# Keys and values of the context attentions: two groups at once, each in seven block products

## The reference

```
q = rope(x @ Wq)        # 512 -> 32 heads x 128
k = rope(ctx @ Wk)      # 512 ->  8 groups x 128
v = ctx @ Wv            # 512 ->  8 groups x 128
p = softmax(q @ k.T / sqrt(128) + mask)   # per batch and head, 128 x 128
x = layernorm(x + (p @ v) @ Wo)
```

## Time and profile before

| | us |
|---|---|
| median of 3 runs | 2557.67 |
| lowest and highest | 2549.81, 2559.54 |
| profiled execution, its own time | 2556.09 |
| span of its instructions | 2554.8 |
| PE busy | 2436.9 (95%) |
| DVE busy | 1671.0 (65%) |
| ACT busy | 989.5 (39%) |
| POOL busy | 733.7 (29%) |

### The profile page before, as it was taken

The page is one execution under the profiler, slowest core; times in us unless marked ns, Lnnn a source line. Parts: engine busy times, 40 slices in busy tenths (PEclk is TensorE's granted clock), DMA queues, the critical chain, the costliest instruction groups (busy, mean ns, idle before and its releaser), DMA issues.

```text
span 2554.8 us, 37687 instructions
## 1 busy us (share of the span) xinstructions
PE 2436.9 (95%) x13016; PEld 1542.3 (60%) x13016; DVE 1671.0 (65%) x3133; ACT 989.5 (39%) x3580; POOL 733.7 (29%) x755
## 2 busy tenths in 40 slices
PE   8999999999999798999999999999998999999998
PEld 7865666666655565456666666556664554555554
DVE  3487777777755777677777777565665644445565
ACT  0013444444444366344444434433555412323330
POOL 1037344443322111364344443222221221000002
PEclk9999999999999999999999999999999999999999
DMA  8452233322322266121333222222661020214430
GB/s 177 101 139 73 76 96 99 87 79 79 93 77 83 91 199 200 62 94 60 95 99 98 89 75 79 87 95 86 191 189 61 22 75 30 95 66 153 132 100 33
DMA packets 220382, 249.97 MB, mean 98 GB/s; under 512 B 49792, under 2 KB 165952, under 8 KB 218144
## 3 DMA queue, kind: packets, MB, share of 16 engines
q1 hardware_dynamic: 212128, 218.20, 28.9%
q10 hardware_dynamic: 8064, 29.36, 3.0%
HBM read 161.49 MB, written 85.98 MB: 97 GB/s over the span
## 4 chain that ended last, share of the span: by engine, by line
PE 80%; DVE 11%; ACT 2%; issue 2%; POOL 2%; DMA 2%; SPq 0%; DVEq 0%; ACTq 0%; POOLq 0%
PE banks L752 12%; PE banks L840 12%; PE banks L824 4%; PE banks L902 4%; PE banks L868 3%; PE banks L303 3%; PE banks L720 3%; PE banks L2091 3%; PE banks L733 3%; PE banks L1521 3%; PE banks L2142 3%; PE banks L2431 2%; PE banks L2468 2%; PE banks L2119 2%; PE banks L2161 2%
## 5 line engine op out<-in xcount | busy, mean ns | idle before, releaser
L947 ACT ACTIVATE E_x<-S_x,sm_x 128x128 f32<-128x128 f32 x512 | 199.2, 390 | 304.3 <-DVE sm_x L1121 304.3
L1183 POOL TENSOR_TENSOR QT<-QT,const 128x512 f32<-128x512 f32 x128 | 171.7, 1342 | 427.7 <-DVE turned L1001 427.7
L161 POOL TENSOR_TENSOR norm_spread<-norm_mv,const 128x1 f32<-128x1 f32 x96 | 20.7, 216 | 909.3 <-DVE norm_mv L157 909.3
L752 PE MATMUL banks<-xT,weights 128*128 128x512 f32 x512 | 237.1, 597 | 7.6 <-POOL weights L1178 5.8
L2589 ACT ACTIVATE E_s<-banks,top_s 128x128 f32<-128x128 f32 x512 | 180.0, 379 | 95.8 <-DVE top_s L2696 95.8
L1079 DVE TENSOR_TENSOR x<-banks,x 128x256 f32<-128x256 f32 (+1 forms) x288 | 147.2, 511 | 84.6 <-PE banks L840 78.6
L840 PE MATMUL banks<-weights,OT 128*128 128x256 f32 x768 | 195.1, 384 | 6.3 <-DVE weights L1062 6.3
L840 PEld LDWEIGHTS banks<-weights,OT 128*128 128x128 f32 x768 | 142.8, 191 | 67.9 <-issue 27.9
L954 ACT ACTIVATE OT<-banks 128x512 f32<-128x512 f32 x128 | 76.1, 595 | 258.2 <-PE banks L902 258.2
L1185 POOL TENSOR_TENSOR QT<-QT,turned 128x512 f32<-128x512 f32 x128 | 169.0, 1320 | 10.0
L752 PEld LDWEIGHTS banks<-xT,weights 128*128 128x128 f32 x512 | 95.0, 191 | 116.5 <-issue 105.6
(11 more groups left out here) (320 smaller groups left out, 4908.1 us busy)
## 6 DMA issues: line engine op xcount, KB each, us to landing
scratch_pt<-blocks_x SPq DMA_DIRECT2D x124, 256.0 KB, 2.0
PT<-scratch_pt SPq DMA_DIRECT2D x496, 64.0 KB, 2.0
scratch_latent_pt<-blocks_s ACTq DMA_DIRECT2D x56, 512.0 KB, 3.6
PT_s<-scratch_latent_pt SPq DMA_DIRECT2D x224, 128.0 KB, 3.0
weights<-in_L_xwq SPq DMA_DIRECT2D x64, 256.0 KB, 3.9
weights<-in_L_xwo SPq DMA_DIRECT2D x64, 256.0 KB, 4.3
scratch_latent_pt<-blocks SPq DMA_DIRECT2D x30, 512.0 KB, 2.6
PT<-scratch_latent_pt SPq DMA_DIRECT2D x120, 128.0 KB, 3.0
```

What stands on the lines that cost most here:

```text
L752: mm = PE.matmul(to, left[:, k, head], moving, start=name in ("P1", "P2", "P4", "P5") and k == 0, stop=k == 1, skip_group_check=name in (" ...
L947: ins = AC.activation(head_of(e, j, u), scores_of(s, j, u), ACT.Exp, bias=sm[:, 0, j:j + 1], scale=1.0, accum_out=sm[:, 1, j:j + 1])
L1183: PO.tensor_tensor(four(to), four(to), spread(cos128, 4), ALU.mult).then_inc(*pool_step.one())
```

## The change

Keys and values are made for two groups at once, as a *pair* job: pair n with even n makes the keys of groups n and n+1, with odd n the values of groups n-1 and n. A pair is cut into the same seven products of blocks as the queries, in three jobs p0 (P2, P1), p1 (P5, P6, P3) and p2 (P4, P7). `Wk` and `Wv` come as 4 matrices of 256 columns. POOL makes three sums of the pair's weights (`pair_sums`, four instructions of 256 elements a partition) for every pair, and once in a stage three sums of ctxT (`sums_of_ctx`, four instructions of 1024 elements a partition); the latter changes ctxT in place, which is why ctxT is loaded again ahead of stage 4 and of the feature attention. ACT copies four blocks of a pair (`pair_copy`: one in p0, two in p1, one in p2), DVE adds four. A product of a pair is two matmuls of 512 positions for keys, and four times two of 128 for values. In the diff, `x_exp(u)` and the like count the units done, and the wait on `x_exp` stands ahead of the mask of unit u. Keys are then rotated from SBUF as queries are. The opening makes pairs 0 and 1; group g makes the queries of g+1 and pair g+2. `S` and `blocks` have one buffer in place of two. The diff, cut to its core (moved waits, views and buffer lists are left out):

```
-            if stage == 1:
-                SP.dma_start(ctxT[:, :, :], dram["ctxT"]).then_inc(*ctx_in.one())
+            SP.dma_start(ctxT[:, :, :], dram["ctxT"]).then_inc(*ctx_in.one())
...
-                S = [sbuf(f"S{n}_x{stage}", [P, 4, P], scope) for n in range(2)]
+                S = sbuf(f"S_x{stage}", [P, 4, P], scope)
-                blocks = [sbuf(f"blocks{n}_x{stage}", [P, 4, P], scope) for n in range(2)]
+                blocks = sbuf(f"blocks_x{stage}", [P, 4, P], scope)
...
-                opening = (("k", 0), ("k", 1)) + QUERIES[0]
-                plans = [(1, 1, 2, 2, 1, 0, 1, 0)] + [(2, 2, 1, 2, 1, 1, 1, 0)] * (G8 - 2)
+                pair_of = [[(0, "p", i) for i in range(3)], [(1, "p", i) for i in range(3)]]
+                q0 = [(0, "q", n) for _, n in QUERIES[0]]
+                opening = pair_of[0][:1] + q0[:4] + pair_of[0][1:] + q0[4:] + pair_of[1]
+                opening_turns = [[], [("k", 0, 0)], [("q", 0, 0), ("q", 0, 1)], [("q", 0, 2)], [("q", 0, 3)], [("k", 0, 1)], [],
+                                 [("q", 0, 4)], [("q", 0, 5)], [("q", 0, 6)], [("q", 0, 7), ("k", 0, 2)], [("k", 0, 3)]]
+                plans = [(1, 1, 2, 1, 1, 1, 1, 1)] + [(1, 2, 1, 1, 1, 1, 1, 1)] * (G8 - 3) + [(1, 1, 1, 1, 1, 1, 0, 0)]
...
+                    jobs = [(g + 1, "q", n) for n in range(6)] + [(g + 2, "p", i) for i in range(3)]
...
-                shares = [(1, 1, 2, 1, 1, 1, 1, 0)] + [(0, 1, 1, 2, 1, 1, 1, 1)] * (G8 - 2)
+                shares = [(1, 1, 1, 1, 1, 1, 1, 1), (2, 2, 1, 2, 1, 2, 1, 1)] * (G8 // 2)
+                def group_turns(g):
+                    keys = [("k", (g + 1) // 2, m) for m in range(4)] if g % 2 else []
+                    return keys + [("q", g + 1, m) for m in range(8)]
...
                  def sp_cross():
...
-                        if b == 2 and g + 2 < G8:
-                            load_keys(g + 2)
-                        if b == 7 and g + 2 < G8:
-                            load_values(g + 2)
                         fetch(u)
+                        if b in (0, 1) and g + 2 < G8:
+                            load_pair(g + 2, slice(2 * b, 2 * b + 2))
...
                  def pe_cross():
...
+                    def pair(n, turn):
...
+                        if turn == 0:
+                            PE.wait_ge(xw_in.sem, w_base + 32 * (n + 1))
+                            if n == 1:
+                                PE.wait_ge(*xp_added(4))
+                            elif n:
+                                PE.wait_ge(*x_qadd(8 * (n - 1) + 8))
+                            product("P2").then_inc(*xp_other.one())
+                            product("P1").then_inc(*xp_main.one())
+                        elif turn == 1:
+                            PE.wait_ge(*xp_sums(n + 1))
+                            PE.wait_ge(*ctx_sums(1))
+                            PE.wait_ge(*xp_here(4 * n + 1))
+                            product("P5").then_inc(*xp_other.one())
+                            PE.wait_ge(*xp_added(4 * n + 1))
+                            product("P6")
+                            PE.wait_ge(*xp_here(4 * n + 2))
+                            product("P3").then_inc(*xp_other.one())
+                        else:
+                            PE.wait_ge(*xp_here(4 * n + 3))
+                            product("P4").then_inc(*xp_other.one())
+                            PE.wait_ge(*xp_added(4 * n + 2))
+                            product("P7").then_inc(*xp_main.one())
...
+                        if n == 0 and g:
+                            PE.wait_ge(*xp_added(4 * (g + 1)))
...
-                    job(0, "k", 0)
                     if stage == 1:
                         before.turn(B - 2)
-                    job(0, "k", 1)
+                    job(*opening[0])
                     before.turn(B - 1)
...
                  def dve_cross():
...
+                    def add_pair(n, turn):
+                        if turn != 1:
+                            DV.wait_ge(*xp_main(2 * n + 1 + turn // 2))
+                        for name in (PAIR_ADDED[0:1], PAIR_ADDED[1:2], PAIR_ADDED[2:4])[turn]:
+                            to = pair_block(n, name)
+                            DV.wait_ge(*xp_here(4 * n + PAIR_OTHER.index(name) + 1))
+                            DV.tensor_tensor(to, psum[0][:, :], to, ALU.add).then_inc(*xp_added.one())
...
                     def turn_blocks(u):
-                        if u >= 2:
-                            DV.wait_ge(*x_kept[u % 2](u // 2))
+                        if u:
+                            DV.wait_ge(*x_kept[(u - 1) % 2]((u - 1) // 2 + 1))
...
                     sums_of_xT(4, B - 1)
                     sums_of_xT(B - 1, B)
+                    for j, turned_here in zip(opening, opening_turns):
+                        drain(*j)
+                        for t in turned_here:
+                            rotate(*t)
                     for step in range(units + 3):
...
-                            if u >= 2:
-                                DV.wait_ge(*x_exp(u - 1))
+                            if u:
+                                DV.wait_ge(*x_exp(u))
...
                  def pool_cross():
...
+                    def sums_of_ctx():
+                        PO.wait_ge(*ctx_in.all())
+                        b11, b12, b21, b22 = ctxT[:, 0:2, 0:HALF], ctxT[:, 0:2, HALF:T], ctxT[:, 2:4, 0:HALF], ctxT[:, 2:4, HALF:T]
+                        PO.tensor_tensor(ctx3[:, :, :], b22, b12, ALU.subtract).then_inc(*pool_step.one())
...
                     PO.wait_ge(*before.added)
                     wq_sums(0)
+                    pair_sums(0)
+                    sums_of_ctx()
+                    for n, turned_here in enumerate(opening_turns):
+                        if n == 9:
+                            pair_sums(1)
+                        for t in turned_here:
+                            rope(t)
+                    wq_sums(1)
+                    for g in range(G8 - 1):
+                        for t in group_turns(g):
+                            if t[0] == "q" and t[2] == 2 and 8 * g < 2 * pairs:
+                                wo_sums(g)
+                            if t[0] == "q" and t[2] == 3 and g + 2 < G8:
+                                pair_sums(g + 2)
+                            if t[0] == "q" and t[2] == 5 and g + 2 < G8:
+                                wq_sums(g + 2)
+                            rope(t)
...
          def load_feature(stage, free):
...
+            SP.dma_start(ctxT[:, :, :], dram["ctxT"]).then_inc(*ctx_in.one())
```

More of the change, by code:

```diff
@@ L797, in job @@
                     def job(g, kind, i):
-                        {"k": keys, "v": values, "q": queries}[kind](g, i)
+                        {"p": pair, "q": queries}[kind](g, i)
                     def products(q, turn):
@@ L936, in act_cross @@
                     AC.wait_ge(*before.added)
-                    for kind, i in opening:
-                        drain(0, kind, i)
-                    for i in range(2):
-                        drain(0, "v", i)
+                    for j in opening:
+                        drain(*j)
                     def exps(u):
-                        s, e, sm = S[u % 2], E[u % 2], small[u % 3]
+                        s, e, sm = S, E[u % 2], small[u % 3]
                         AC.wait_ge(*x_top(u + 1))
@@ L1181, in rope @@
+                    def rope(t):
+                        j, to = turn_index[t], turn_target(*t)
                         PO.wait_ge(*x_taken(j + 1))
-                        if cosines:
-                            PO.tensor_tensor(four(to), four(to), spread(cos128, 4), ALU.mult).then_inc(*pool_step.one())
-                            PO.wait_ge(*pool_step.all())
+                        PO.tensor_tensor(four(to), four(to), spread(cos128, 4), ALU.mult).then_inc(*pool_step.one())
+                        PO.wait_ge(*pool_step.all())
@@ L1188, in pool_cross @@
                     wq_sums(0)
-                    for g in range(G8):
-                        for i in range(2):
-                            rope(NR * g + i, KT[g % 2][:, half_of(i)], False)
-                        for m in range(8):
-                            if m == 5 and 1 <= g < G8 - 1:
-                                wq_sums(g + 1)
-                            if m == 2 and 1 <= g and 8 * (g - 1) < 2 * pairs:
-                                wo_sums(g - 1)
-                            rope(NR * g + 2 + m, query(g, *rotated(g)[m]), True)
-                        if g == 0:
-                            wq_sums(1)
+                    pair_sums(0)
[15 more added lines that the diff above has]
+                            rope(t)
                     for b in range(B):
```

212 lines of the change are left out of this document (110 added, 102 removed).

## The result

The changed kernel takes 2699.8 us (2695.1 to 2705.2) beside 2553.7 (2545.2 to 2559.5) for the kernel before: ratio 1.0563, 95% interval 1.0542 to 1.0584. The forecast was 2612, with 2645 as its upper end: the direction was right, and the loss of 146 us is two and a half times the forecast one.

What follows compares the result with a forecast made beforehand. PE was taken to bound the kernel, with DVE and POOL hardly keeping up in the opening. 2556.1 - 21.0 (saving) + 48.4 (openings) + 18 (turn 1) + 11 (DVE) = 2612 us; range 2553 to 2645.

Steps and rivals of the forecast that it cites:

- The saving: Pairs outside the openings: seven products in place of eight save PE 1.75 us a pair, 21.0 us over 12 pairs.
- The opening: Both stages' openings: PE waits for sums of xT, `pair_sums(1)` and `wq_sums(1)`; 24.2 us lost each, +48.4 (22 to 58).
- The rule of the Trainium skill: Two-input DVE and SBUF-reading GpSimd instructions exclude each other; opening sums of xT 1.5 us later, 2615 in place of 2612.
- Turn 1 as first job: First jobs q1, q4, p1: P3 waits half a microsecond for ACT's copy behind the exponentials, 18 times a stage; +18 (0 to 25).
- DVE in groups 1, 3, 5: DVE's extra turns fit on average (70 of 76 us) but make single steps 1.8 us late; +11 (0 to 43).
- The clock: Opening: PE's P1 of pair 1 runs at the lower clock behind an 8 us wait, costing 1.7 us more.
- Nothing for `S`, `blocks` and ctxT: Single buffers for `S` and `blocks` and loading ctxT again were claimed to cost nothing.

Runs made afterwards that it cites:

- spread turns and copy first: Changed kernel with ten rotations in every group, `wo_sums` earlier, two opening rotations left out, and ACT's first copy of turn-1 jobs ahead of the exponentials: 2581.6 us.
- the last run: Spread turns and copy first, most opening pair jobs moved into group 0, rotations reordered, `pair_sums(1)` ahead of group 0's late rotations: 2557.9 us, 1.0011 to before.
- `wo_sums` early: Changed kernel with POOL making the output weights' sums ahead of query block 1's rotation in groups 1, 3 and 5: 2699.9 us.
- the fill: Changed kernel with six extra PE products, read by nobody, ahead of the first output product of groups 1, 3 and 5: 2691.9 us.
- the late pairs: Spread turns and copy first, with all pair 0 and 1 jobs but the first moved from opening to group 0, DVE making context sums: 2607.1 us.

## Why the prediction was wrong

**The saving** was right in PE's work and overrated in time. Forecast 77.42 - 1.75 = 75.67 for a full group; with spread turns and copy first, PE is busy 76.09 and 75.58. But the groups last 77.0 and 76.5, since the first output products of a group still wait 0.34 for `wo_sums` and 0.57 for `ot_sums`. In the last run PE is busy 24.3 us less than before, and the time is the same: PE's idle time is 22.8 us longer (2553.3 - 2412.6 against 2554.8 - 2436.9), in many short waits.

**The opening** was right: 26.8 and 27.1 for 24.2, by the walked chain. The last sum of xT came at 190.25, so 189.0 against the stage's start for the 188 forecast; POOL's sums of 1024 elements took 2.34 to 2.66 (forecast 2.54), those of 256 between 0.72 and 1.17 (0.64). PE came to q1 at 181.8 against the stage's start and not at 176.5 to 179, which changed nothing, since the sums came later still. The lower clock lies behind all three waits, and one was priced. DVE's timeline beside POOL's sums:

```profile
181.81 2.43 DVE L1082 TENSOR_TENSOR weights<-xT 128x128 f32<-128x128 f32 x1
184.16 0.28 DVE L1084 TENSOR_TENSOR xT<-xT 128x128 f32<-128x128 f32 x1
184.47 2.31 DVE L1085 TENSOR_TENSOR weights<-xT 128x128 f32<-128x128 f32 x1
```

One sum that takes 0.28 alone lasts 2.3 to 2.4 while POOL reads SBUF, and a second one slips in at most. The rule of the Trainium skill, "SBUF — State Buffer", § Who interferes with whom, holds here: with it the prediction would have been 1.5 us a stage later, and 1.0 was measured.

**Turn 1 as first job** had the right mechanism and less than half its size: 18 forecast, 44.0 us of waits (18.2 + 15.4 + 10.4), and 42 us by undoing it. The half microsecond was read from a step in which DVE came in time; behind a double turn the mask, and so the exponentials and the copy, come later (1.88 for q1, 2.80 for p1 in group 1, 0.23 for q4 behind a single turn). p1 of the even groups waits 1.97 behind a single turn, whose two instructions in group 2 took 1.13 and 1.67 us there.

**DVE in groups 1, 3, 5** is the step that failed. "I take the one that I can work out: 6 x 1.8 = +11" counted a lag against the next third product alone. The double turn at the end of step 3 was named there, "beside wo_sums", but nobody was asked who waits behind it: PE's first output product, for `wo_sums` by way of POOL's rotations, and for `ot_sums` by way of DVE itself. The wait for `wo_sums` was put at nothing in the sum; it is 5.64 to 5.70 us in each of the six odd groups of the two stages, 34.0 us in all, and was not there before. The second chain hides behind the first: the 7.9 us of waits for `ot_sums` fall in groups 0, 2 and 4, and only with `wo_sums` early does it show in the odd groups, as 3.25 us in each, so that shortening one chain alone gave nothing. The upper bound of 43 covered the waits and not the lower clock behind them.

**The clock** was priced once, 1.7 us, in the opening. It was lower behind each of the 5.64 us waits of the odd groups too, and behind some of those of 2.80 and 1.88 us: 50 us of PE's busy time in all. How much of it is on the path stays open; the fill brought 7.9 us, not clear of the spread.

**Nothing for `S`, `blocks` and ctxT** was right: 0.9996.

In sum: openings 54 for 48; the groups about +92 (146 - 54) for the forecast -21 + 18 + 11 = +8. By what PE does: 119.8 us more of waits and 25.8 more of busy time, which is 28 less of products and 54 of the same products drawn out. Undoing the order of turns and copies takes 118 off, and moving the opening's work another 24. What stays open is which of the small waits keep the last version from being faster than before; none of them was taken up by itself.

## What to carry to other kernels

An average load of 70 of 76 us says nothing of a step with two long instructions at its end: for each, list what is queued behind it on its own engine and on the engine that it feeds, and which instruction of the bound engine waits there. When a wait is undone and the time stays, look at the next releaser before dropping the cause: two chains may hang on the same instruction. Give each prepared value a due time (the step that reads it), and make it neither in the step ahead of that nor all at once in an opening.

## What the runs showed of the hardware that was not expected

Waits of the same length were followed by either level of TensorE's clock. In the changed kernel p1 waits 2.80 us in groups 1, 3 and 5 of stage 1, and the granted clock of the 3.5 us behind it was 0.51, 0.55 and 1.00 (1.00 is the level of 2.4 GHz, 0.50 that of 1.2; the first and the last are shown above). q1 waits 1.88 us in the same groups, and the clock behind it was 1.00, 0.67 and 1.00. Windows of group 3, behind q1 and behind p1:

```profile
504.30:507.80 3.50, 3.48 (x7) 1.89 (x8) 0.17 (x1) 0.60 (x1) 0.00 (x0) 0.67 0.32 82
566.60:570.10 3.50, 3.50 (x17) 3.50 (x18) 0.85 (x2) 0.00 (x0) 3.42 (x3) 0.55 0.83 204
```

With the six fill products some 20 us ahead, the three waits of p1 were followed by 1.00, 0.59 and 0.50. So neither a wait's own length nor the filled stretch ahead settled its price here.

VectorE made a sum of 1024 elements in 1.22 us while GpSimd stood still (timeline of the late pairs' opening); GpSimd took 2.34 to 2.66 for one in the changed kernel:

```profile
199.13 1.22 DVE L1103 TENSOR_TENSOR ctx_sum<-ctxT 128x1024 f32<-128x1024 f32 x1
200.39 1.22 DVE L1104 TENSOR_TENSOR ctx_sum<-ctxT,ctx_sum 128x1024 f32<-128x1024 f32 x1
```
